# A chained eight-layer transformer step on one core: a merged weight built earlier, and the turns that leave a convolution stack reordered

## Time and profile before

| | |
|---|---|
| three runs | 1317.97, 1323.69, 1324.55 us; median 1323.69 |
| profiled execution | 1323.85 us; span 1322.1 us; mean granted clock 0.976 |
| PE busy | 1241.2 us, 94% of the span |
| DVE, ACT, POOL busy | 714.1 (54%), 437.1 (33%), 162.2 us (12%) |
| 238.4 to 326.3 us (layer 2, merging) | PE busy 80.5 of 87.9, clock 0.92 |
| 326.3 to 370 us (layer 3) | PE busy 42.6 of 43.7, clock 1.00 |
| 710 to 768 us (exit of layer 5, layer 6) | PE busy 52.1 of 58, clock 0.89 |

### The profile page before, as it was taken

The page is one execution under the profiler, slowest core; times in us unless marked ns, Lnnn a source line. Parts: engine busy times, 40 slices in busy tenths (PEclk is TensorE's granted clock), DMA queues, the critical chain, the costliest instruction groups (busy, mean ns, idle before and its releaser), DMA issues. The chain is left out here.

```text
span 1322.1 us, 14300 instructions
## 1 busy us (share of the span) xinstructions
PE 1241.2 (94%) x5333; PEld 843.1 (64%) x5344; DVE 714.1 (54%) x1186; ACT 437.1 (33%) x747; POOL 162.2 (12%) x215
## 2 busy tenths in 40 slices
PE   7899999899998999998888899899999988999998
PEld 4788688544576788787564445455555533688886
DVE  4321545367748666454343658677767734334344
ACT  2121422111121124222323223466656566222221
POOL 0000000000068200102111220011112224000000
PEclk9999999799999999999977999999999999999999
DMA  8010001733234551103000010000000001022001
GB/s 341 32 49 15 0 1 38 307 127 118 72 109 177 214 214 48 46 0 135 0 0 1 0 48 1 1 1 2 2 2 1 2 3 49 3 94 71 0 25 40
DMA packets 18264, 79.06 MB, mean 60 GB/s; under 512 B 3104, under 2 KB 3872, under 8 KB 16032
## 3 DMA queue, kind: packets, MB, share of 16 engines
q1 hardware_dynamic: 18208, 78.32, 16.4%
HBM read 75.95 MB, written 2.10 MB: 59 GB/s over the span
## 5 line engine op out<-in xcount | busy, mean ns | idle before, releaser
L2348 DVE TENSOR_REDUCE mqa_top<-psum 128x1 f32<-128x512 f32 (+3 forms) x304 | 186.6, 657 | 50.9 <-PE psum L2140 28.4
L2255 ACT ACTIVATE mqa_prob<-psum 128x512 f32<-128x512 f32 x288 | 156.7, 603 | 83.4 <-PE psum L2170 79.4
L587 PE MATMUL psum<-L_ffn_x,L_ffn_w_up 128*128 128x512 f32 x624 | 145.4, 394 | 7.2 <-DVE L_ffn_hidden L740 6.1
L587 PEld LDWEIGHTS psum<-L_ffn_x,L_ffn_w_up 128*128 128x128 f32 x624 | 117.6, 190 | 34.9 <-DVE L_ffn_hidden L740 8.6
L587 PE MATMUL psum<-L_attn_x,L_attn_w_up 128*128 128x512 f32 x456 | 105.4, 393 | 3.9 <-DVE L_attn_hidden L740 3.9
L587 PEld LDWEIGHTS psum<-L_attn_x,L_attn_w_up 128*128 128x128 f32 x456 | 86.6, 190 | 22.5 <-issue 4.3
L2170 PE MATMUL psum<-mqa_stack_back,mqa_keys 100*128 100x512 f32 x208 | 96.2, 462 | 0.9 <-DVE mqa_stack_front L2339 0.9
L2183 PE MATMUL psum<-mqa_prob,mqa_v 128*32 128x512 f32 x576 | 78.4, 609 | 0.0
L117 ACT ACTIVATE ln_std<-ln_mean_var,eps 128x1 f32<-128x1 f32 x56 | 16.5, 295 | 179.2 <-DVE ln_mean_var L104 179.2
L2077 POOL TENSOR_SCALAR_AFFINE_SELECT mqa_prob<-mqa_prob 128x512 f32<-128x512 f32 x64 | 41.7, 671 | 255.5 <-ACT mqa_prob L2255 255.2
L2170 PEld LDWEIGHTS psum<-mqa_stack_back,mqa_keys 100*128 100x128 f32 x208 | 40.0, 192 | 50.2 <-ACT mqa_prob L2255 41.9
(11 more groups left out here) (299 smaller groups left out, 2051.8 us busy)
## 6 DMA issues: line engine op xcount, KB each, us to landing
L_ffn_stage<-in_L_w SPq DMA_DIRECT2D x25, 768.0 KB, 4.7
L_ffn_z_int<-in_L_z SPq DMA_DIRECT2D x14, 768.0 KB, 4.4
L_ffn_s_all<-in_L_s SPq DMA_DIRECT2D x14, 768.0 KB, 6.1
lora_wo<-in_L_wo SPq DMA_DIRECT2D x8, 1024.0 KB, 6.0
L_attn_stage<-in_L_w SPq DMA_DIRECT2D x10, 512.0 KB, 3.5
L_attn_w_down<-in_L_down SPq DMA_DIRECT2D x1, 2560.0 KB, 24.3
x_feat<-in_x_feat SPq DMA_DIRECT2D x2, 1024.0 KB, 6.9
x_tok<-in_x_tok SPq DMA_DIRECT2D x1, 2048.0 KB, 18.7
```

The source lines that it names most:

```text
L587: ins = nc.tensor.matmul(bank[place][:, :], w_up[:, slot, w_part, at:at + P], x_half[half][:, x_part, k, :], start=k == 0 and n == 0, stop ...
L2255: nc.scalar.activation(prob[:, n % PROBS, :], score_bank[n % 3], ACT.Exp, scale=SCALE)\
L2348: nc.vector.tensor_reduce(top[:, i % 2, 2 if lo == qt * P else lo // HALF, heads[0]:heads[-1] + 1], max_bank[n % 3][:, 0:len(heads) * widt ...
```

## The change

- The head sums and their loads move from layer 2/3's block into layer 1's: a class `MergedHeads` with two slots of `wo`, pair sums in place, one head behind each norm of tiles 1 to 6 (heads 0 to 5), heads 6 and 7 behind layer 2's tiles 0 and 2. Loads go out when `split_h` has read the hidden tiles that lay there, or when a slot's sum is done; `wv` in front of `expert.load`, head 6's load behind it.
- For this, `hidden` and `terms` are laid out by token tile, so that memory is freed tile by tile; the number of elements of each operation stays the same.
- The 32 merging products are dealt out: 4 at the end of layer 1, 2 after the mean's products, 1 after the last transposes, 3 after the scores, 2 after the expert products, then 8, the transposes, and 12. The entry's small products move to banks 4 to 7; the last expert group then waits for the last tile's copy.
- `Rotation.dve` goes ahead of the adds to `w_eff`, `Rotation.act` ahead of layer 2's roots. Layer 4's first tile is dequantised behind tile 5, the second ahead of the copies to `w_values` instead of within layer 3's loop.
- `conv_stack`: 4 dummies ahead of the last two transposes, 2 behind them, 4 behind the first two output products; each later output product is issued one turn earlier.

```diff
@@ FfnRoom
+        self.by_tile = not quantised
-        self.hidden = sb("hidden", [P, tiles, TOK], F32)
+        self.hidden = sb("hidden", [P, NT, tiles, P] if self.by_tile else [P, tiles, TOK], F32)
...
@@ swiglu, sync
                 if expert is not None:
+                    for g in range(6):
+                        heads.load_heads(sp, a, g)
+                    heads.load_values(sp, a)
                     expert.load(sp, a, extra_split)
+                    heads.load_heads(sp, a, 6)
@@ swiglu, tensor
                 if expert is None:
                     tail.pe(pe, NT - 1)
+                else:
+                    heads.products(pe, range(KC))
@@ swiglu, vector
                     if expert is not None and t == NT - 1:
-                        expert.add_tokens(dve, tail, t - 1)
+                        for earlier in (t - 2, t - 1):
+                            expert.add_tokens(dve, tail, earlier)
                     tail.dve(dve, t)
+                    if heads is not None and 1 <= t < NT - 1:
+                        heads.add_heads(dve, t - 1)
+                    if expert is not None and 2 <= t < NT - 1:
+                        expert.add_tokens(dve, tail, t - 2)
                     if t + 2 < NT:
                         split_h(dve, t + 2, 0, 1)
-                    if expert is not None and 1 <= t < NT - 1:
-                        expert.add_tokens(dve, tail, t - 1)
...
+class MergedHeads:
+    KV, SLOTS, STEPS = 8, 2, 8 * KC
...
+    def load_heads(self, sp, a, g):
+        if g < self.SLOTS:
+            sp.wait_ge(self.h_lo, 4 * (g + 1))
+        else:
+            sp.wait_ge(self.summed, g - self.SLOTS + 1)
+        sp.dma_start(self.wo[:, g % self.SLOTS, :, :], a["L1_wo"][g]).then_inc(self.wo_loaded[g % self.SLOTS], 16)
+    def load_values(self, sp, a):
+        sp.wait_ge(self.h_lo, 14)
+        sp.dma_start(self.wv[:, :, :], a["L1_wv"]).then_inc(self.wv_loaded, 16)
+    def add_heads(self, dve, g):
+        four = self.wo[:, g % self.SLOTS, :, :]
+        dve.wait_ge(self.wo_loaded[g % self.SLOTS], 16 * (g // self.SLOTS + 1))
+        self.c.nc.vector.tensor_tensor(four[:, 0:2, :], four[:, 0:2, :], four[:, 2:4, :], ALU.add)\
+            .then_inc(self.paired, 1)
+        dve.wait_ge(self.paired, g + 1)
+        self.c.nc.vector.tensor_tensor(self.wo_sum[:, g, :], four[:, 0, :], four[:, 1, :], ALU.add)\
+            .then_inc(self.summed, 1)
...
@@ lora_then_single_key, sync
-                for g in range(KV):
...
+                heads.load_heads(sp, a, heads.KV - 1)
@@ lora_then_single_key, tensor (the mean, the query, the transposes, the scores)
+                heads.products(pe, range(4, 6))
...
+                heads.products(pe, range(6, 7))
...
+                heads.products(pe, range(7, 10))
                 pe.wait_ge(w_loaded, 32)
                 for i in range(KC):
+                    if i == KC - 1:
+                        pe.wait_ge(entry.tail.feat_ready, entry.tail.base + NT)
...
-                pe.wait_ge(entry.tail.feat_ready, entry.tail.base + NT)
+                heads.products(pe, range(10, 12))
...
+                heads.products(pe, range(12, 20))
+                tail.pe(pe, NT - 1)
+                heads.products(pe, range(20, heads.STEPS))
@@ lora_then_single_key, scalar
                 entry.tail.act_copy(act, NT - 1)
+                c.rot.act(act)
                 tail.act(act)
-                c.rot.act(act)
                 if start is not None:
                     start.high(act, 0)
+                    start.high(act, 1)
@@ lora_then_single_key, vector
-                add_heads(0)
+                c.rot.dve(dve)
                 dve.wait_ge(org_loaded, 16)
...
                 for t in range(NT):
                     tail.dve(dve, t)
-                    if t in (2, 4, 6, 7):
-                        add_heads(3 + (2, 4, 6, 7).index(t))
-                add_heads(7)
-                if start is not None:
-                    start.room.dequantise(dve, 0, 0, True)
-                c.rot.dve(dve)
+                    if t in (0, 2):
+                        heads.add_heads(dve, 6 + t // 2)
+                    if start is not None and t == 5:
+                        start.room.dequantise(dve, 0, 0, True)
                 if start is not None:
                     start.low(dve, 0)
+                    start.room.dequantise(dve, 1, 1, True)
+                    start.low(dve, 1)
@@ conv_stack, tensor
+                keep_busy(4)
                 transposes(2 * C_DEPTH, 0)
                 transposes(2 * C_DEPTH, 1)
+                keep_busy(2)
...
+                out(0)
+                out(1)
+                keep_busy(4, 3)
+                for t in range(1, NT + 3):
                     if 1 <= t <= NT:
                         tail.pe(pe, t - 1)
+                    if 2 <= t + 1 < NT:
+                        out(t + 1)
                     if 2 <= t < NT + 2:
                         pe.wait_ge(tail.feat_ready, tail.base + t - 1)
                         product_tiles(c, pe, tail_two, two.w_eff, t - 2)
```

More of the change, by code:

```diff
@@ L326, in __init__, with hidden_half, half_of, hidden_tile @@
         self.wd = wd
+    def hidden_half(self, f, half):
+        if self.by_tile:
+            return self.hidden[:, half * NT // 2:(half + 1) * NT // 2, f, :]
+        return self.hidden[:, f, half * HALF:(half + 1) * HALF]
+    def half_of(self, bank):
+        return bank.rearrange("p (t n) -> p t n", n=P) if self.by_tile else bank
+    def hidden_tile(self, t, group):
+        if self.by_tile:
+            return self.hidden[:, t, group.start:group.stop, :]
+        return self.hidden[:, group.start:group.stop, t * P:(t + 1) * P]
     def dequantise(self, dve, f, slot, first, pieces=(0, 1)):
@@ L423, in swiglu @@
            extra_dve=None, extra_pe=None, extra_act=None, extra_split=None, table=None, ahead=None, a=None,
-           start=None, expert=None):
+           start=None, expert=None, heads=None):
     nc = c.nc
@@ L469, in split_h @@
         def split_h(engine, t, g, part):
[L471 removed]
+            src = room.hidden_tile(t, groups[g])
             n, u = len(groups[g]), 2 * t + g
@@ L860, in products, with gradient_ffn @@
         ins.then_inc(self.used, 1)
-def gradient_ffn(c, a, entry):
+def gradient_ffn(c, a, entry, heads):
     nc = c.nc
@@ L966, in gradient_ffn @@
                extra_loads=loads, extra_dve=make_terms,
-               extra_pe=(project, series), extra_act=ratios, extra_split=split, expert=entry, a=a)
+               extra_pe=(project, series), extra_act=ratios, extra_split=split, expert=entry, heads=heads, a=a)
 def product_tiles(c, pe, tail, w, t, chunks=KC):
@@ L1023, in lora_then_single_key @@
+def lora_then_single_key(c, a, front, start, entry, heads):
     nc = c.nc
     E, R, K, RC = entry.E, entry.R, entry.K, entry.RC
-    KV, PER, SLOTS = 8, 4, 3
     with ExitStack() as own:
@@ L1153, in _ @@
                         tail_values.act_copy(act, t - 1)
-                    if start is not None and t == 3:
-                        start.high(act, 1)
                 tail_values.act_copy(act, NT - 1)
@@ L1230, in _ @@
                         tail_values.dve_low(dve, t - 1)
-                    if start is not None and t in (1, 2):
-                        start.room.dequantise(dve, 1, 1, True, (t - 1,))
-                    if start is not None and t == 4:
-                        start.low(dve, 1)
                 if start is not None:
@@ L2419, in build @@
         entry = ExpertEntry(c, 16992)
-        gradient_ffn(c, a, entry)
+        heads = MergedHeads(c, 131488)
+        gradient_ffn(c, a, entry, heads)
         c.rot = Rotation(c)
```

116 lines of the change are left out of this document (56 added, 60 removed).

## The result

Measured on one chip, the kernel before took 1320.85 us (median of four runs) and the changed one 1302.85 us (1300.54 to 1310.21): a ratio of 0.9867 with an interval of 0.9822 to 0.9912. The forecast was 1304.6 in a range of 1298 to 1314. A second comparison on another chip gave 0.9893 (0.9856 to 0.9930), 1304.95 us.

What follows compares the result with a forecast made beforehand. PE, busy for 94% of the span, was taken as the bound, through its work, idle time and clock. 6.2 + 5.4 - 1.4 + 1.1 + 8.0 = 19.3 us off 1323.85 gave 1304.6 us, range 1298 to 1314.

Steps and rivals of the forecast that it cites:

- Part 1: Layer 1: head sums and loads fit DVE's idle 4.84 us per tile; cost 0, bounds minus 0.2 and plus 2 us.
- Part 2: Entry: twelve merging products dealt into PE's gaps gain 6.2 us of idle time and 5.4 us of clock.
- Part 3: DVE order in entry and layer 3: new stall of 1.4 us at tile 6, 1.1 us gained in layer 3.
- fit by 0.4: Entry's end: ACT and DVE work through three chunk copies, about 10.0 us, fits PE's 10.4; cost 0, bounds 0 and 3.
- Rotation 0: Rotation on DVE beside the expert products: cost 0, about 1 us in hand, at most 12 us without cover.
- Part 4: Exit of layer 5: dummies and earlier output products gain 8.0 us together, bounds 3 and 9.
- The first part: Exit, from the last transposes to the end of the first like product: 12.6 us, 2.6 gained.
- The rule against it: Exit: a two-port DVE operation and a GpSimd operation exclude each other, so denser turns could meet POOL's add each time.
- The rival's 1.26 in each turn: Exit: POOL's add blocks a norm for up to 1.26 us per turn, 2.8 us over five, 1307.4; chance alone 0.07.
- both places named: Rival: clock falls all the same, in the exit (1309.6), the entry (1310) or both (1315); chance 0.20.
- DVE became no bound: Rival: DVE becomes the bound through late rotation, second dequantise meeting copies, or POOL's add; 1307.4 or 1310, chance together 0.13.
- layer 4's loads: Rival: layer 4's dequantise waits for its first loads, so 10.2 us saved return as a wait; 1315 to 1318, chance 0.05.

Runs made afterwards that it cites:

- The added dummies: Changed kernel with four dummies more between the two groups of transposes at the head of each of layer 5's four blocks; ratio to the kernel before 0.9826.

## Why the prediction was right, point by point

**The total.** The forecast was 19.3 us off the time before. The stages named gave 19.04, the medians 18.0 in the first comparison and 13.65 in the second. That the time itself came within 1.8 us of the forecast is in part luck: the kernel before had a median of 1320.85 in the comparison, 2.84 below the 1323.69 that the forecast starts from, and this made up for a gain 1.3 smaller than forecast.

**Part 1.** Cost 0, measured 0: the six tiles take 73.16 us before and after. The step held by its size, not in each detail. I had looked at the loads of heads 2 to 5; it is head 1's, gated by the splits of tile 3, that comes 2.18 us late, and the row sum of 0.61 us, now in the same gap, isn't in the sum either. Together they stayed 0.2 us under the 2.99 that the sums leave, so in this tile the cost of 0 was a near thing, and in part luck.

**Part 2.** Gaps 6.2: measured 6.56 - 0.30 = 6.26, the hand-over as taken. (The 0.83 at 266.76, taken as its bound, is not a hand-over between blocks: PE waits there for DVE's last add to the effective matrix, which ends at 266.67.) Clock 5.4: mean 0.81, query 0.90, transposes 0.46, scores 0.16 (not in the forecast), experts 3.04, together 5.37. The guess that the mean and query products halve was the weakest term; 1.02 and 0.95 for 0.92 say it was right. The merging in one run gives most of these 11.6 back: its gaps are 6.20 more than the changed kernel's, its clock costs 3.79 (less than before in that execution: 15.72 for 16.94 and 1.47 for 1.83), and it lost 10.35.

**Part 3.** The stall at tile 6: 1.4 forecast, a gap of 1.26 measured, and 1.48 gained where it was taken away. The copies "fit by 0.4": they fit by 0.17. Layer 3: 1.1 forecast, 1.30 measured, the gap of 0.90 with it; no run moved the second dequantise back by itself, so that this is its doing is argued, not shown. Rotation 0: in the new place the last add to the effective matrix waits 0.30 us for PE, so DVE is on time; and the price without that cover, put at up to 12 us, was 11.0 by layer 4's start. That the two are so near is chance: the 11.0 hold 3.07 of lost clock and some 3.7 by which waiting for ScalarE makes the chain longer, and the 12 had neither.

**Part 4.** 8.0 forecast, 7.57 measured. The first part, 12.6 us to the end of the first product, took 12.9; five turns of 5.16 in place of 6.06 and one output product fewer are 5.3 of the 5.4. What the first part lacked is mostly a gap of 0.25 us behind the four dummies; the 1.2 taken for the wait for norm 1 was 1.13. The runs split the gain otherwise than the prediction, 4.43 for the order and 3.11 for the dummies in place of 5.4 and 2.6, since at the low clock the new order makes the first part longer (16.0 us without the dummies; in the kernel before 15.2).

**The rule against it.** POOL's add now does meet a norm in four turns (0.68 us each). DVE, then POOL, in the changed kernel's exit:

```profile
720.94 0.68 DVE L111 TENSOR_SCALAR x_tok<-x_tok,ln_mean_var,ln_rstd 128x512 f32<-128x512 f32 x1
...
724.40 0.69 DVE L97 TENSOR_TENSOR x_tok<-x_tok,psum 128x512 f32<-128x512 f32 x1 [0.58 <-PE psum L1004]
...
720.08 1.26 POOL L1636 TENSOR_TENSOR x_tok<-x_tok,two_bias 128x512 f32<-128x512 f32 x1 [3.90 <-PE psum L153]
```

The norm takes 0.68 in place of 0.55 and ends 0.28 us after POOL's add, and DVE still waits 0.58 for PE. The rival's 1.26 in each turn didn't come. The Trainium skill, page "SBUF — State Buffer", section "Who interferes with whom", has a DVE operation in a two-port mode and a GpSimd operation exclude each other: whoever issues first holds the shared ports for its whole instruction, and the other blocks. If all of the norm's 0.55 us had to follow POOL's add, it would run from 721.34 to 721.89; the row ends at 721.62. In the kernel before, where the prediction read its 0.22 us as agreeing, it would have ended at 719.75; the row ends at 719.49. So the rows agree with a wait, but with a shorter one. Which part of the norm can run beside the add, or whether POOL's recorded end is late, no run here shows; it costs nothing here.

**The rivals.** The clock stayed at full in both places named; DVE became no bound but at tile 6; layer 4's loads were on time (layer 3 has 0.3 us of idle PE). Where the clock did fall, in the rest of layer 5, it fell before the change too, and I had counted that stretch as unchanged: 101.38 us before, 100.53 and 103.50 in the changed kernel's two profiles.

## What to carry to other kernels

Where PE stands still behind short chains and long independent products follow, deal the products into the gaps: in the entry half of the gain was the gap (6.26 us) and half the clock that no longer fell behind it (5.37). To make such products independent, find an earlier stage in which the other engine idles, and size what you put there by its idle time in one turn, with the late load in the sum. A long chain of tiny operations is moved like any other work: here its place, on DVE and ScalarE, decided over 11.0 us.

## What the runs showed of the hardware

The clock of a stretch with short products and waits isn't the same in two executions of one program. Layer 5's stretch took 98.03 us (in the kernel with the two-piece dequantise), 100.53 and 103.50 us (in the changed kernel's two profiles) with the same instructions in it; the granted clock was 0.97, 0.93 and 0.90. The added dummies held it at 1.00 from the second block on. What decides it at the start of layer 5, where PE waits 1.10 us at the hand-over in each of them, wasn't tried.
